# A layer seam in a four-layer transformer kernel: the POOL queue's drain replaced by a signalled memset, and two loads of expert rows asked for ahead of eleven others

## The reference

```python
# layer 0, feed-forward: two of eight experts for each token
sorted_xs = x_flat[xs_indices, :]
gate_out = ragged_dot(sorted_xs, w_gate, group_sizes=tokens_per_expert)
activation = gelu(gate_out[:, 0, :]) * gate_out[:, 1, :]
expert_outputs = ragged_dot(activation, linear, group_sizes=tokens_per_expert)
out = expert_outputs[xs_reverse_argsort].reshape((G, S, k, -1))
out = einsum('blkd,blk->bld', out, combine_weights)

# layer 1, attention: 16 heads of 32, with a second, small set of keys and values
kv_dca = (y_dca @ Wkv_dca + bkv_dca).reshape(b, DCA, 2, H, HD)
k_dca = _ln(kv_dca[:, :, 0], kn_dca_w, kn_dca_b)
q = _ln((x @ Wq + bq).reshape(b, s1, H, HD), qn_w, qn_b)
kv = concatenate([y_main @ Wk + bk, y_main @ Wv + bv])
k = _ln(kv[..., :HD], kn_w, kn_b)
ctx = _attn(q, k, v) + DCA_WEIGHT * _attn(q, k_dca, v_dca)
return ctx @ Wo + bo
```

## Time and profile before

| | us |
|---|---|
| median of 3 runs | 3827.72 |
| lowest and highest run | 3822.49, 3834.49 |
| the profiled execution | 3825.5 |
| its span in the profile | 3822.6 |
| PE busy in it | 3421.7 (90%) |
| DVE busy | 2420.4 (63%) |
| POOL busy | 1288.1 (34%) |

### The profile page before, as it was taken

One profiled execution on the slowest core, in us unless ns is written; L12 is line 12 of the kernel. 1 busy time (PEld: TensorE's weight loads), 2 busy tenths in 40 slices (PEclk: granted clock), 3 DMA queues, 4 the chain that ended last, 5 costly groups with the idle time before them and its releaser, 6 DMA issues.

```text
span 3822.6 us, 62015 instructions
## 1 busy us (share of the span) xinstructions
PE 3421.7 (90%) x23446; PEld 2805.6 (73%) x23446; DVE 2420.4 (63%) x4746; ACT 1623.7 (42%) x3496; POOL 1288.1 (34%) x1212
## 2 busy tenths in 40 slices
PE   5999999958999489997999789998779999999977
PEld 5899999947777256655998545554579999999865
DVE  6778888863322378865443446665566777777766
ACT  3566665431111055551222245555145555555431
POOL 0003334102241477742222346665322222222212
PEclk9999999988999799998999989999899999999989
DMA  3236665114644200001010100000000000000001
GB/s 121 75 116 220 222 221 191 42 61 163 253 170 162 77 26 28 22 5 56 34 45 1 37 3 4 4 3 15 20 17 12 18 18 18 7 18 18 12 1 47
DMA packets 94468, 246.52 MB, mean 64 GB/s; under 512 B 14432, under 2 KB 18656, under 8 KB 89312
## 3 DMA queue, kind: packets, MB, share of 16 engines
q1 hardware_dynamic: 87936, 222.12, 16.8%
q0 software_dynamic: 6240, 20.45, 1.5%
HBM read 364.95 MB, written 70.52 MB: 114 GB/s over the span
## 4 chain that ended last, share of the span: by engine, by line
PE 37%; DVE 6%; issue 3%; POOL 2%; ACT 2%; DMA 1%; SPq 0%; POOLq 0%; DVEq 0%; ACTq 0%
PE banks L100 33%; PE banks L203 4%; ACT P L74 1%; POOL rs L83 1%; DVE XL L83 0%; DVE xn L88 0%; POOL kst L83 0%; DVE X L83 0%; POOL X L83 0%; DVE X L91 0%; DVE st L240 0%; DVE P L87 0%; DVE PL L83 0%; ACT nkT L77 0%; DVE KL L91 0%
## 5 line engine op out<-in xcount | busy, mean ns | idle before, releaser
L83 DVE TENSOR_TENSOR X<-X,banks 128x512 f32<-128x512 f32 x352 | 239.9, 683 | 203.1 <-PE banks L100 202.9
L94 DVE TENSOR_REDUCE nmx<-banks 128x4 f32<-128x1024 f32 (+2 forms) x256 | 239.2, 955 | 158.5 <-PE banks L100 155.3
L100 PE MATMUL banks<-XH,wqh 128*128 128x256 f32 x1024 | 291.8, 285 | 0.0
L100 PE MATMUL banks<-XL,wqh 128*128 128x256 f32 x1024 | 286.1, 279 | 0.0
L100 PE MATMUL banks<-XH,wql 128*128 128x256 f32 x1024 | 285.9, 279 | 0.0
L83 POOL TENSOR_TENSOR slo<-sraw,shi 128x512 fp32r<-128x512 f32 x96 | 126.4, 1316 | 471.9 <-ACT shi L77 465.8
L100 PE MATMUL banks<-XH,tT 128*128 128x256 f32 x1024 | 248.1, 286 | 13.7 <-issue 6.6
L100 PE MATMUL banks<-XL,tT 128*128 128x256 f32 x1024 | 246.7, 284 | 0.0
L74 ACT ACTIVATE nPT<-banks 128x1024 f32<-128x1024 f32 x192 | 195.9, 1020 | 110.2 <-PE banks L100 108.5
L100 PE MATMUL banks<-woh,OH 128*128 128x512 f32 x512 | 219.9, 429 | 11.9 <-DVE OL L83 10.2
L74 ACT ACTIVATE P<-banks,nb,qst 128x256 f32<-128x256 f32 x256 | 141.2, 561 | 190.6 <-DVE nb L83 190.6
(11 more groups left out here) (425 smaller groups left out, 10551.8 us busy)
## 6 DMA issues: line engine op xcount, KB each, us to landing
WU<-expert_parts SPq DMA_DIRECT2D x39, 4096.0 KB
WD<-expert_parts SPq DMA_DIRECT2D x39, 2048.0 KB
sraw<-in_moe_w SPq DMA_DIRECT2D x96, 256.0 KB, 3.2
expert_parts<-shi SPq DMA_DIRECT2D x96, 256.0 KB
expert_parts<-slo SPq DMA_DIRECT2D x96, 256.0 KB
wqr<-in_L_xattn_Wq SPq DMA_DIRECT2D x16, 512.0 KB, 3.5
wor<-in_L_xattn_Wo SPq DMA_DIRECT2D x16, 512.0 KB, 4.7
sraw<-in_L_ffn_factors SPq DMA_DIRECT2D x32, 256.0 KB, 3.1
```

The source lines that it names most:

```text
L83: return self.e.tensor_tensor(out, a, b, op)
L94: return self.e.tensor_reduce(out, a, AX.X, op, **kw)
L100: return self.e.matmul(out, l, r, start=start, stop=stop, skip_group_check=skip)
```

## The change

POOL no longer drains its queue at fence 2. A new method, `pool_leave_experts`, issues the memset of nom that stood in the preparation, lets that memset signal the fence when it is done, and waits for the fence as before. nom moves behind nos and no in SBUF, to an address that the experts' tables don't use, since it is now written before the fence. The memset and its wait at L1786 go, and the count of n_sel is one lower. SP issues the eleven loads in the step behind the first two ngt loads instead of ahead of the wait for the scatters.

```diff
@@ the counts for layer 2 @@
-            ... "n_xa": 16, "n_xb": 16, "n_sel": 11}
+            ... "n_xa": 16, "n_xb": 16, "n_sel": 10}
@@ narrow_tiles @@
-            for k in self.B1 + ("om", "os", "o1"):
+            for k in self.B1 + ("os", "o1", "om"):
                 sb(k, [128, 32], F32)
@@ sp_narrow @@
             if step == "gl":
                 sp.wait_ge(S["gsum"], 3 * (a - 2) + 1)
                 sp.dma(w["gt"][:, a % 2, :, :], back[a]).then_inc(S[f"x{2 + a % 2}"], 16)
+                if a == 1:
+                    self.sp_narrow_load(sp, 1)
@@ new @@
+    def pool_leave_experts(self, pool):
+
+        pool.e.memset(self.W[1]["om"][:], 1.0).then_inc(self.S["fence"], 1)
+        pool.wait_ge(self.S["fence"], 10)
+
@@ pool_narrow @@
         if l1:
-            pool.e.memset(w["om"][:], 1.0).then_inc(S["n_sel"], 1)
-            pool.wait_ge(S["n_sel"], c + 1)
             pool.e.affine_select(out=w["os"][:, 0:16], in_=w["om"][:, 0:16], compare_op=ALU.is_ge, fill=0.0, base=111,
                                  pattern=[[0, 16]], channel_multiplier=-1)
@@ pool_program @@
         self.pool_experts(pool)
-        self.fence(pool, 2)
+        self.pool_leave_experts(pool)
         pool.count_on(EXPERTS)
@@ sp_program @@
         self.fence(sp, 2)
-        self.sp_narrow_load(sp, 1)
         sp.wait_ge(S["back"], 16 * NBLK)
```

More of the change, by code:

```diff
@@ L51 @@
             "n_eq": 103, "n_ek": 103, "n_st": 64, "n_sc": 64, "n_e": 64, "n_mx": 128, "n_pv": 32, "n_mt": 32, "n_mT": 32,
-            "xs0": 2048, "xs1": 1792, "n_o": 32, "n_r": 96, "n_y": 16, "n_vv": 16, "n_xa": 16, "n_xb": 16, "n_sel": 11}
+            "xs0": 2048, "xs1": 1792, "n_o": 32, "n_r": 96, "n_y": 16, "n_vv": 16, "n_xa": 16, "n_xb": 16, "n_sel": 10}
 class Eng:
```

## The result

| | before | with the change |
|---|---|---|
| median, us | 3828.57 (20 runs) | 3820.13 (20 runs) |
| lowest and highest run | 3820.1, 3834.49 | 3815.46, 3832.55 |
| ratio, 95% interval | | 0.998 (0.9974 to 0.9986) |

The change takes 0.20% off, about 7.7 us, with an interval from 5.4 to 10.0. The forecast was 15.7. The gain is real and half as large as predicted, and the median lies 0.1 us beyond the upper end of the range given (3804 to 3820). By the bound given above (0.3%) it counts as no difference.

The account below looks back on a forecast made before the run. The prediction took a serial chain at the seam between experts and layer 1 (scatter, drain, eleven issues, load, adds, PE) as the bound; 3827.7 - 15.7 = 3812 us, range 3804 to 3820.

Parts of the forecast that it names:

- The seam: Between the experts and layer 1: POOL's add into X, and PE behind it, comes 15.7 us earlier (bound 15.4).
- The drain goes, a memset stands in its place: At fence 2: nom's memset follows the last scatter at once and opens the fence 6.3 us earlier.
- What follows: Layer 1 and later: the whole pattern moves up alike by 15.7 us; clock stretching may shift it 3 us either way.
- POOL pays the 6.4 us anyway: Rival at fence 2: nom would still start 6.55 us late; gain only 9.2, 3818.5 us; chance 0.08.
- The second term, the fill: Layer 1's fill: 3 us either way from the clock; rival of 4 us or more, 3808 or 3816, chance 0.11.
- a lead changed by 1400: Sign of being wrong: the 15.7 us lead at 1294 has shrunk or grown by time 1400 in layer 1.
- The loads behind: Eleven loads issued after two ngt loads: nwd and ncd still in time for PE at 1283.4, cost nothing.
- the rule of the ring: Loads taken in ring order: two ngt transfers would delay ncd by 2.6 us, making the gain 15.2, not 15.7.
- third ngt: SP's third ngt load goes out 1.0 us late, lands by 1288.5 against POOL's need at 1288.7: costs nothing.
- The rivals of late loads, 3 us or 15: PE waits for ncd: 3 us late gives 3815 us, chance 0.12; 15 us late starts a loss, slower chance 0.01.
- no slowdown would come: Whole kernel: a loss of over 0.3%, 3839 us or more, was given chance 0.01.

Follow-up runs that it names:

- number 3: The change with the eleven loads issued ahead of the ngt loads again, behind the wait for the scatters: 3831.11 us, ratio 1.0009 to the kernel before.
- number 4: The kernel before, its drain kept, with only the eleven loads moved behind the first two ngt loads: 3820.44 us, ratio 0.9981.
- number 5: The changed kernel plus a POOL drain in layer 1 behind its last add into OT, where POOL waits for DVE: 3814.91 us, ratio 0.9961.
- numbers 2: The changed kernel run again with no edit, for a second profile: 3821.62 us, ratio 0.9982 to the kernel before.
- number 9: The changed kernel plus a POOL drain behind the scatter of block 18 in the experts' loop: 3816.95 us, ratio 0.9968 to the kernel before.
- 10: The changed kernel plus a POOL drain behind the scatter of block 36 in the experts' loop: 3814.26 us, ratio 0.996 to the kernel before.
- number 6: The kernel before plus a second POOL drain behind the scatter of block 36, near the experts' end: 3822.6 us, ratio 0.9984.
- number 7: The changed kernel with the added layer 1 drain, plus unused PE products in the seam's pause and the fill's waits: 3804.13 us, ratio 0.9935.

## Why the prediction was half right

**The seam: right, term by term.** The chain of scatter, drain, eleven issues, load, two adds and nxn was what held PE, and its parts were priced right: nom at once, ngt out 3.24 us after the scatter (3.3), landed in 3.7 (3.7), POOL's add at 7.91 (8.0) with its own preparation as the last releaser, the pause 15.85 shorter (15.7). The two halves apart fit too: by number 3, 4.2 without the new order (4.1 expected); by number 4, 9.3 without the new exit (9.3). They add up to less than 15.85, because in each half the part left as it was still holds POOL's first add.

**The step that failed** is "The drain goes, a memset stands in its place", together with "What follows", which said that no later operation of layer 1 waits for anything that has a time of its own. The drain of fence 3 was such a thing: the prediction took the drain as a wait of fence 2 alone and priced its work at nothing anywhere else. It was in the trace, 1362 ns long and just ahead of DVE, and I had read fence 1's 1394 only as "no scatter ahead". Both were short because none of the experts' 78 DMAs was unpaid there: they come behind fence 1, and fence 2's drain stood between them and fence 3. The rival "POOL pays the 6.4 us anyway" had the right price and the wrong place: I let it fall only on POOL's next instruction, saw the add 0.03 us behind a scatter speak against it, and gave it 0.08. No operation of layer 1 pays; the next drain does, 480 us later: 6.4 us more in the drain (7758 against 1362 ns), 5.7 more in the lag, and both gone again in number 5. That rival's 3818.5 came near the result by another road. Of the code load that the Trainium skill names in "GPSIMD Engine Reference", "Instruction dispatch", no run here shows a sign: nom starts with no delay, and a price that goes with the number of DMAs since the last drain doesn't look like one of a first call.

**The second term, the fill, was mis-sized.** I allowed 3 us either way and put 0.11 on 4 or more. Its sign was left open, though the trace had a reason for one: what follows the seam had run at 0.71 and 0.82, so it had something to lose from how its work meets the low clock. The sign of being wrong that the prediction named, a lead changed by 1400, came: DVE's seventh add stands 106.5 us behind PE's first transpose before, and 112.1 and 107.8 in the two profiles after. The four kernels that keep the changed fill and have the 15.0 pause, with no products added (numbers 2, 5, 9, 10), took 84.9, 85.0, 83.0 and 84.8, and the first profile 89.2: a mean of 85.4, 1.8 more than the 83.6 that the kernel before shows both times, and number 6 too.

**The balance.** Pause -15.85, lag +5.7 (the mean of two), fill +1.8: -8.4 us, against -7.7 (5.4 to 10.0) measured. With the debt hidden, numbers 5 and 10 have -15.85, +0.2 and +1.3: -14.4, against -14.9 and -15.3 by their ratios (interval of each some 5 either way). So 15.7 lies within what this change brings with the debt paid in idle time. That the measured gain is near half of it is chance: debt and fill happen to add up so, and the fill alone moved by 4.4 between two profiles of the change.

**The loads behind: right.** PE did not wait for nwd or ncd. As the prediction priced the rule of the ring, 2.6 us would have been added to ncd's landing; its time from issue to landing stayed at 8.0. SP's third ngt, behind the eleven, took 10.0 us instead of 3.7, from 1283.13 to 1293.1; POOL wanted it at 1296.73, so it cost nothing. The rivals of late loads, 3 us or 15, did not come. That no slowdown would come held for the whole change, but number 3 shows that one half of it is no gain.

**Left open.** What POOL does in the debt's time. Gathers and scatters seem to cost alike: the 39 and 39 of fence 3 after the change and the 15 and 20 of number 9 are solved by 0.081 us for a gather and 0.083 for a scatter. Why one kernel's fill differs between executions (89.2 and 84.9) while the kernel before repeats to 0.1 us. Where it differs can be seen: between DVE's third and fifth add into X, 34.8 us in the long fill and 30.8 in the short one, as these windows of the first and the second profile show (columns as for the fill):

```profile
1314.38:1349.21 34.83, 22.06 (x42) 8.77 (x40) 17.50 (x29) 6.20 (x14) 29.15 (x21) 0.71 0.09 31
```
```profile
1312.35:1343.18 30.83, 17.98 (x42) 7.35 (x40) 17.85 (x29) 6.21 (x14) 28.79 (x20) 0.83 0.12 39
```

Number 9's drain holds POOL 3.7 us behind block 18's scatter, and no cost of it is to be seen at the end of the experts: from that scatter to the last one are 188.4 us, and 186.8 to 191.2 in the other kernels. Layer 1's fill at 1.00 behind the kernel before's 30.8 pause was not tried.

## What to carry to other kernels

A wait that you remove is gone only if nothing else has to do its work: before you count it as a gain, find the next place where the same engine is asked to finish, and whether that place is free. A POOL that has sent many DMAs should be drained where it idles anyway, not at a fence where all wait. And a stage that is moved is not moved rigidly where PE has gaps: compare its length and granted clock in both traces, and price PE's gaps by what the next products cost at the low clock in the trace.

## What the runs showed of the hardware

- **A POOL drain costs some 0.082 us for each DMA that POOL issued since its last drain**, and 0.10 besides, however late it comes. Behind the work just ahead of it: 6.4 to 6.5 us for 78 (fence 2 before, fence 3 after), 6.3 for 76, 3.6 for 43, 2.98 for 35, 0.28 for 2, 0.10 for none. These are gathers and scatters of 128 rows. The other POOL operations behind a scatter didn't pay it (nom starts as the scatter ends).
- **The clock can be worth more than a removed wait.** The same fill took 75.6 us at a mean granted clock of 1.00, 82.5 at 0.86, 83.0 to 85.0 at 0.81 to 0.83 (within which the mean clock doesn't order them: 83.6 at 0.81, 84.9 at 0.82), and 89.2 to 89.4 at 0.75 to 0.77. Products that compute nothing, in PE's waits, took about 10 us off the program (number 7 against number 5).
